# Expert first layers of two MoE blocks as pairs in the upper and lower half of TensorE's rows

## The chip, the cores and the metric

The kernel runs on one core of one Trainium2 chip. The metric is the device time of one execution in microseconds (us). TensorE (PE) multiplies, with its weight loads listed as PEld; VectorE (DVE), ScalarE (ACT) and GpSimd (POOL) do the elementwise work, SyncE (SP) issues the DMAs. PE has two clock levels, 1.2 and 2.4 GHz; the profile gives the granted clock as a share of the higher one.

## What is computed

A network of four blocks on an image batch x of shape (8, 32, 32, 64), float32, each a token mixer followed by an expert layer, with normalizations and residuals: a selective-scan mixer and dense experts; a sum-product layer and a top-2 expert layer; a sum-product layer and an LSTM; a depthwise convolution with attention and a last expert layer. The two expert layers whose first layers the change touches, and the LSTM beside which they run, are, cut to what matters:

```python
# block 1: dense experts, E = 8, 64 -> 64 -> 64 -> 64
h = jnp.einsum('bfd,edh->bfeh', x, W1) + b1
h = jax.nn.relu(_bn(h, g1, be1, m1, v1))
h = jnp.einsum('bfeh,ehk->bfek', h, W2) + b2
...
return jnp.einsum('bfed,fe->bfd', y, w)

# block 2: top-2 of 8 experts, 64 -> 128 -> 64
h = jax.nn.gelu(xf @ w1 + bb1, approximate=False)
y = h @ w2 + bb2
return (acc + we[:, None] * y, None)

# block 3: LSTM over 512 steps of a sequence, hidden size 64
i_t = jax.nn.sigmoid(xi_t + h @ V_i)
f_t = jax.nn.sigmoid(xf_t + h @ V_f)
g_t = jnp.tanh(xg_t + h @ V_c)
o_t = jax.nn.sigmoid(xo_t + h @ V_o)
c_new = h * c + i_t * g_t
h_new = o_t * jnp.tanh(c_new)
```

## The kernel before

The image is cut into 32 tiles of one image row for all 8 batches: 256 tokens, held as two groups of 128 partitions. In the first 2600 us the tiles go through a software pipeline of `turns`. In one turn each stage works on another tile: the two halves of the mixer (`block0`, `block1`) lead, the dense experts (`ffn0_*`, stage ffn) are 3 tiles ahead of the LSTM, the top-2 experts (`mix_*`, stage mix) 2 tiles, and the convolution's 49 taps (L1152) are 5 tiles behind it, so they begin five turns later. The LSTM's turn has 32 steps, each needing the step before. After this phase come the attention and the last expert layer, which the change leaves as they are.

The order of instructions on every engine is static. Each stage is a generator that yields between pieces; `weave` (L1215) merges the stages of a turn by the due times in `TIMES` (from L78), one row of numbers for each stage and engine, in half steps of the LSTM. The LSTM yields its own: its matmuls, its first tanh and the scan at t - 0.5, the second tanh and r_h at t. A piece that is due at 6 thus stands behind the matmuls of LSTM step 6 and ahead of those of step 7.

A step t of the LSTM is, by lines: three gate matmuls (L1047, L1048, L1049) read r_h and add to psL; ACT takes tanh of the gates (L1058, L1060); DVE scans the cell state (L1072); ACT takes its tanh (L1063); DVE writes the new r_h (L1077), and a scaled copy (L1079). In the text, "interval 4 to 5" is the time from the matmuls of step 4 to those of step 5 (steps are counted from 0).

The expert layers: `ffn0_pe` transposes the normalized tile f_xn (L710) into psB[0:64], ACT copies it to f_xT (L744), and the first layer multiplies it by four blocks of 128 weight columns, two experts of 64 each (L720), into the two banks of psB; ACT's relu (L755) follows. `mix_pe` does the same for m_xn (L911, ACT's copy at L952), with eight experts of 128 columns (L929) in the two banks of psC: experts 0 and 1 in bank 0, 2 and 3 in bank 1, 4 and 5 in bank 0, 6 and 7 in bank 1; ACT's gelu (L962) follows and needs its function table loaded each time. The inputs have 64 channels: partitions 64 to 127 of f_xT and m_xT hold zeros, set once, and the matmuls use all 128 rows (with `w128`, whose lower half is other data). psA belongs to the mixer, psL to the LSTM and the convolution. W holds all packed weights; a DMA named `w_late` brings those of the expert layers.

## Time and profile before

| quantity | before |
| --- | --- |
| runs | 3163.59, 3164.37, 3166.41 us; median 3164.37 |
| profiled execution | span 3157.1 us |
| PE busy | 2771.7 us, 88% |
| PEld busy | 2231.2 us, 71% |
| DVE busy | 1953.5 us, 62% |
| ACT busy | 1668.0 us, 53% |
| POOL busy | 874.9 us, 28% |
| a turn of the pipeline with convolution | about 72.7 us |

The span is the time between the first and the last instruction of the one execution that was profiled; the run times are those of other executions and include what lies around the span. A busy share is an average over stages with different limits: the pipeline of the first 2600 us has PE busy in almost all of it, the attention and the last expert layer less. In a timeline a row gives the start in us, the duration, the engine, the line, the operation, output and inputs with their shapes (for a matmul ahead of these the tile of the array, rows*columns), how many alike are merged in the row, and in brackets the idle time ahead of it and what ended that. An fp32 matmul leaves two records, an fp32 transpose one.

### The profile page before, as it was taken

How to read it: one execution, taken by the hardware profiler on the slowest of the kernel's cores; microseconds unless marked ns; L12 is line 12 of the kernel's file. 1: busy time of each engine (PE TensorE's matmuls, PEld its weight loads, DVE VectorE, ACT ScalarE, POOL GpSimd, SP SyncE). 2: the span in 40 equal slices, each digit the busy share in tenths (PEclk: the TensorE clock that was granted, in tenths of full speed). 3: DMA queues.
4: the chain of work that ended last, by engine and by line, in shares of the span. 5: the costliest groups of instructions: out<-in, count | busy, mean ns of one | idle time of the engine just before them, and what ended most of it. 6: DMA issues, size and time to landing. Idle time of an engine off the chain costs nothing. (4 is left out here: it accounts for less than half of the span.)

```text
span 3157.1 us, 64810 instructions
## 1 busy us (share of the span) xinstructions
PE 2771.7 (88%) x22240; PEld 2231.2 (71%) x22240; DVE 1953.5 (62%) x8535; ACT 1668.0 (53%) x5755; POOL 874.9 (28%) x1499
## 2 busy tenths in 40 slices
PE   4477888899999999999999999999998787887667
PEld 3366666678888788888888888788777564555556
DVE  5466666676667677777766667677754324555454
ACT  1245555566666666666665666666654423443333
POOL 2233222233233333323333333333311000000444
PEclk8677766688888888888888888888886688998888
DMA  2000000000000100000000000000000001000000
GB/s 100 14 17 18 18 19 19 19 19 19 21 21 20 32 19 19 19 19 19 19 19 19 21 21 25 27 19 19 19 17 9 3 2 28 1 1 1 8 10 11
DMA packets 54039, 59.12 MB, mean 19 GB/s; under 512 B 26576, under 2 KB 45136, under 8 KB 53328
## 3 DMA queue, kind: packets, MB, share of 16 engines
q1 hardware_dynamic: 53712, 54.99, 6.0%
q8 instruction: 177, 2.90, 0.4%
q14 instruction: 150, 1.23, 0.1%
HBM read 42.37 MB, written 4.19 MB: 15 GB/s over the span
## 5 line engine op out<-in xcount | busy, mean ns | idle before, releaser
L1072 DVE TENSOR_TENSOR_SCAN r_c<-r_wk 64x24 f32<-64x24 f32 x1024 | 244.3, 239 | 490.4 <-ACT r_wk L1058 486.5
L1058 ACT ACTIVATE r_wk<-psL 64x16 f32<-64x16 f32 x1024 | 189.1, 185 | 678.1 <-PE psL L1048 659.9
L1152 PE MATMUL psL<-img,dg 128*128 128x128 f32 x2646 | 452.7, 314 | 0.0
L1047 PEld LDWEIGHTS psL<-r_h,lv 128*64 128x64 f32 x2048 | 235.6, 162 | 291.1 <-DVE r_h L1077 162.9
L1047 PE MATMUL psL<-r_h,lv 128*64 128x8 f32 x2048 | 324.6, 231 | 80.6 <-DVE r_h L1077 74.8
L1152 PEld LDWEIGHTS psL<-img,dg 128*128 128x128 f32 x2646 | 378.4, 215 | 11.8 <-issue 3.9
L1049 PE MATMUL psL<-r_h,lv 128*64 128x8 f32 x2048 | 326.4, 232 | 0.0
L1048 PE MATMUL psL<-r_h,lv 128*64 128x8 f32 x2048 | 304.7, 222 | 0.0
L1077 DVE SCALAR_TENSOR_TENSOR r_h<-r_wk,r_tc 64x8 f32<-64x8 f32 x1024 | 196.3, 192 | 115.0 <-ACT r_tc L1063 101.5
L1063 ACT ACTIVATE r_tc<-r_c 64x8 f32<-64x8 f32 x1024 | 215.5, 210 | 83.8 <-DVE r_c L1072 37.7
L1048 PEld LDWEIGHTS psL<-r_h,lv 128*64 128x64 f32 x2048 | 252.7, 171 | 0.0
L1079 DVE SCALAR_TENSOR_TENSOR r_wk<-r_h,r_c 64x8 f32<-64x8 f32 x1024 | 223.8, 219 | 35.5
L1049 PEld LDWEIGHTS psL<-r_h,lv 128*64 128x64 f32 x2048 | 232.2, 160 | 0.0
L678 POOL TENSOR_TENSOR a_xw<-a_S,a_dtm 128x512 f32<-128x512 f32 x128 | 150.5, 1204 | 188.1 <-DVE a_dtm L591 188.1
L1060 ACT ACTIVATE r_wk<-psL 64x8 f32<-64x8 f32 x1024 | 181.7, 177 | 24.7
L929 PE MATMUL psC<-m_xT,W 128*128 128x256 f32 x512 | 167.3, 421 | 0.0
L451 PE MATMUL psA<-a_xw,a_RM 128*32 128x64 f32 x2048 | 133.1, 230 | 18.8 <-DVE state L628 17.2
L755 ACT ACTIVATE f_h<-psB,bn0b,bn0s 128x256 f32<-128x256 f32 x256 | 132.7, 556 | 8.1 <-PE psB L720 5.9
L669 POOL TENSOR_TENSOR a_bc<-W,a_S 128x128 f32<-128x128 f32 x128 | 49.5, 407 | 309.0 <-DVE a_S L565 302.0
L451 PEld LDWEIGHTS psA<-a_xw,a_RM 128*32 128x32 f32 x2048 | 113.5, 116 | 30.2 <-issue 25.9
L944 PEld LDWEIGHTS psC<-W,m_h 128*128 128x128 f32 x1024 | 130.2, 193 | 1.8
L823 PE MATMUL psC<-c_eT,accb 128*64 128x18 f32 x1024 | 129.5, 273 | 0.0
(376 smaller groups left out, 6558.8 us busy)
## 6 DMA issues: line engine op xcount, KB each, us to landing
accb<-acc_in SPq DMA_DIRECT2D x64, 512.0 KB, 4.3
a_xy<-a_E SPq DMA_DIRECT2D x512, 16.0 KB, 1.8
W<-pack_in SPq DMA_DIRECT2D x1, 3165.0 KB, 13.7
x6d<-X SPq DMA_DIRECT2D x64, 32.0 KB
out_x<-X SPq DMA_DIRECT2D x32, 64.0 KB, 1.6
X<-x_in SPq DMA_DIRECT2D x1, 1856.0 KB, 17.7
W<-pack_in SPq DMA_DIRECT2D x1, 1331.0 KB, 5.8
X<-x_in SPq DMA_DIRECT2D x1, 192.0 KB
```

The source lines that it names most:

```text
L451: last = nc.tensor.matmul(bk[TT * j:TT * j + TT].rearrange("p (b h d) -> p h b d", b=B4, h=NH)[:, h], u["RM"][:, j * NH + h], u["xw"][:, j ...
L929: last = nc.tensor.matmul(psC[:, e // 2 % 2, (e % 2) * 256:(e % 2 + 1) * 256], w128("m1w1", e * P, (e + 1) * P), u["xT"][:], start=True, s ...
L1047: nc.tensor.matmul(psL[0:64, par, c:c + LB], lv[:, 0], h, start=False, stop=False, skip_group_check=True)
L1048: nc.tensor.matmul(psL[0:64, par, c + LB:c + 2 * LB], lv[:, 1], h, start=False, stop=False, skip_group_check=True).then_inc(sem("r_z"), 1)
L1049: nc.tensor.matmul(psL[64:P, par, c:c + LB], lv[:, 2], h, start=False, stop=False, skip_group_check=True).then_inc(sem("r_zo"), 1)
L1058: nc.scalar.activation(o, psL[0:64, par, c:c + 2 * LB].rearrange("p (g b) -> p g b", b=LB), ACT.Tanh).then_inc(sem("r_gi"), 1)
L1060: nc.scalar.activation(TO, psL[64:P, par, c:c + LB], ACT.Tanh)
L1063: nc.scalar.activation(r_tc[:], r_c3[:, t % 2, 2::3], ACT.Tanh, scale=0.5).then_inc(sem("r_tc"), 1)
L1072: v.tensor_tensor_scan(r_c3[:, t % 2, :], r_wk[:, 0:24], r_wk[:, 30:54], 0.0, ALU.mult, ALU.add).then_inc(sem("r_c"), 1)
L1077: v.scalar_tensor_tensor(r_h[0:64, t + 1], TO, 1.0, r_tc[:], ALU.add, ALU.mult).then_inc(sem("r_hr"), 1)
L1079: v.scalar_tensor_tensor(r_wk[:, 32:56:3], r_h[0:64, t + 1], 0.5, r_c3[:, t % 2, 2::3], ALU.mult, ALU.mult).then_inc(sem("r_hc"), 1)
L1152: last = nc.tensor.matmul(o, dg[:, ky * KT + kx], rows[:, :, ky, kx:kx + IMG], start=(n == 0), stop=(n == KT * KT - 1))
```

## The change

The transposed tile is written twice: beside each transpose into partitions 0 to 63, a matmul with the identity writes the same into partitions 64 to 127, and ACT copies all 128 partitions. Three DMAs, issued by SP once `w_late` has landed, write weights of half of the experts into the partitions 64 to 127 that lie beside the others' weights; DVE's set-up waits for them (`w_dup`), and two memsets of the zeros leave. Each pass over the first layer is then two matmuls of 64 rows: one in rows 0 to 63 that writes bank 0, one in rows 64 to 127 that writes bank 1. For the dense experts there are two such pairs in place of four matmuls; for the top-2 layer four pairs in place of eight: experts (0,2), (1,3), (4,6), (5,7). A pair takes two due times of the table, whose numbers are unchanged, and stands at the second of them. The semaphores that tell ACT of finished banks now come with the second pair of a group, for both banks; the waits for the gate's results (f_ld, m0_ld) stand before the first pair, and the wait for a free bank before pair (4,6).

```diff
+LOWER_HALF = (("f0w1", 0, 2 * P), ("m1w1", 0, 2 * P), ("m1w1", 4 * P, 6 * P))
...
@@ ffn0_pe
             for j in range(J):
-                last = nc.tensor.transpose(psB[0:64, 0, j * P:(j + 1) * P], f_ln["xn"][:, j], ident)
+                nc.tensor.transpose(psB[0:64, 0, j * P:(j + 1) * P], f_ln["xn"][:, j], ident)
+                last = nc.tensor.matmul(psB[64:P, 0, j * P:(j + 1) * P], f_ln["xn"][:, j], ident, start=True, stop=True)
...
-            for q in range(4):
+            for q in range(2):
                 yield
-                if q == 2:
+                yield
+                if q == 0:
                     pe.wait_ge(sem("f_ld"), i1)
-                last = nc.tensor.matmul(psB[:, q // 2, (q % 2) * 256:(q % 2 + 1) * 256], w128("f0w1", q * P, (q + 1) * P), xT, start=True, stop=True)
-                if q % 2:
-                    last.then_inc(sem("f_mm1"), 1)
+                for bank in range(2):
+                    r = slice(64 * bank, 64 * bank + 64)
+                    last = nc.tensor.matmul(psB[:, bank, q * 256:(q + 1) * 256], w128("f0w1", q * P, (q + 1) * P)[r], xT[r], start=True, stop=True)
+                    if q:
+                        last.then_inc(sem("f_mm1"), 1)
@@ ffn0_act
-            nc.scalar.activation(f_xT[0:64].rearrange("p b t -> p (b t)"), psB[0:64, 0, 0:256], ACT.Copy).then_inc(sem("f_xTs"), 1)
+            nc.scalar.activation(f_xT[:].rearrange("p b t -> p (b t)"), psB[:, 0, 0:256], ACT.Copy).then_inc(sem("f_xTs"), 1)
@@ mix_pe
             for j in range(J):
-                last = nc.tensor.transpose(psC[0:64, 0, j * P:(j + 1) * P], u["ln"]["xn"][:, j], ident)
+                nc.tensor.transpose(psC[0:64, 0, j * P:(j + 1) * P], u["ln"]["xn"][:, j], ident)
+                last = nc.tensor.matmul(psC[64:P, 0, j * P:(j + 1) * P], u["ln"]["xn"][:, j], ident, start=True, stop=True)
...
-            for e in range(E):
+            for e in (0, 1, 4, 5):
                 yield
-                if e == 2:
+                yield
+                if e == 0:
                     pe.wait_ge(sem("m0_ld"), i1)
-                if e in (4, 6):
-                    pe.wait_ge(sem("m0_h"), 4 * i + (e // 2 - 1))
-                last = nc.tensor.matmul(psC[:, e // 2 % 2, (e % 2) * 256:(e % 2 + 1) * 256], w128("m1w1", e * P, (e + 1) * P), u["xT"][:],
-                                        start=True, stop=True)
-                if e % 2:
-                    last.then_inc(sem("m0_mm1"), 1)
+                if e == 4:
+                    pe.wait_ge(sem("m0_h"), 4 * i + 2)
+                for bank in range(2):
+                    r = slice(64 * bank, 64 * bank + 64)
+                    last = nc.tensor.matmul(psC[:, bank, (e % 2) * 256:(e % 2 + 1) * 256], w128("m1w1", e * P, (e + 1) * P)[r], u["xT"][r],
+                                            start=True, stop=True)
+                    if e % 2:
+                        last.then_inc(sem("m0_mm1"), 1)
@@ mix_act
-            nc.scalar.activation(u["xT"][0:64], psC[0:64, 0, 0:256], ACT.Copy).then_inc(sem("m0_xTs"), 1)
+            nc.scalar.activation(u["xT"][:], psC[:, 0, 0:256], ACT.Copy).then_inc(sem("m0_xTs"), 1)
@@ SP
+            sp.wait_ge(sem("w_late"), 16)
+            for name, upper, lower in LOWER_HALF:
+                at = COL[name][1]
+                sp.dma_start(W[64:P, at + upper:at + upper + 2 * P], pack_in[0:64, at + lower:at + lower + 2 * P]).then_inc(sem("w_dup"), 16)
@@ DVE set-up
-            v.memset(f_xT[64:P], 0.0)
-            v.memset(mix1["xT"][64:P], 0.0)
...
+                dve.wait_ge(sem("w_dup"), 16 * len(LOWER_HALF))
```

PE, around LSTM steps 4 and 5, where the dense experts' first layer stands; before, one of the four L720 is ahead of step 4 and three are behind it:

```order
L720 MATMUL psB<-f_xT,W 128x256
L1047 MATMUL psL<-r_h,lv 64x8 [waits r_hr]
L1048 MATMUL psL<-r_h,lv 64x8
L1049 MATMUL psL<-r_h,lv 64x8
L720 MATMUL psB<-f_xT,W 128x256
L720 MATMUL psB<-f_xT,W 128x256 [waits f_ld]
L720 MATMUL psB<-f_xT,W 128x256
L406 MATMUL psA<-W,hb 128x128 [waits a1_ve]
```

PE at the same place after (lines have moved by 1 to 9: the LSTM's matmuls are L1056 to L1058, the mixer's L406 is L407):

```order
L1056 MATMUL psL<-r_h,lv 64x8 [waits r_hr]
L1057 MATMUL psL<-r_h,lv 64x8
L1058 MATMUL psL<-r_h,lv 64x8
L725 MATMUL psB<-f_xT,W 128x256 [waits f_ld]
L725 MATMUL psB<-f_xT,W 128x256 x3
L407 MATMUL psA<-W,hb 128x128 [waits a1_ve]
```

All four matmuls, the two pairs, now stand behind step 4, and the wait for f_ld is ahead of all of them.

PE from LSTM step 11 to step 13, with the last expert matmuls of the top-2 layer (L736 is the dense experts' last layer, L1152 the convolution, L435 and L439 the mixer), before:

```order
L929 MATMUL psC<-m_xT,W 128x256 [waits m0_h]
L736 MATMUL psB<-W,f_h 128x128 x2
L1152 MATMUL psL<-img,dg 128x128 x3
L929 MATMUL psC<-m_xT,W 128x256
L929 MATMUL psC<-m_xT,W 128x256 [waits m0_h]
L435 MATMUL psA<-state,a_ct 128x128 [waits a1_ve]
L435 MATMUL psA<-state,a_ct 128x128
L1047 MATMUL psL<-r_h,lv 64x8 [waits r_hr]
L1048 MATMUL psL<-r_h,lv 64x8
L1049 MATMUL psL<-r_h,lv 64x8
L929 MATMUL psC<-m_xT,W 128x256
L439 MATMUL psA<-a_xy,a_bc 64x128 x2
```

And after, from the same place:

```order
L741 MATMUL psB<-W,f_h 128x128 x2
L1161 MATMUL psL<-img,dg 128x128 x3
L938 MATMUL psC<-m_xT,W 128x256 [waits m0_h]
L938 MATMUL psC<-m_xT,W 128x256
L436 MATMUL psA<-state,a_ct 128x128 [waits a1_ve]
L436 MATMUL psA<-state,a_ct 128x128
L1056 MATMUL psL<-r_h,lv 64x8 [waits r_hr]
L1057 MATMUL psL<-r_h,lv 64x8
L1058 MATMUL psL<-r_h,lv 64x8
L938 MATMUL psC<-m_xT,W 128x256 x2
L440 MATMUL psA<-a_xy,a_bc 64x128 x2
```

Ahead of step 12 three experts (4, 5 and 6) became the pair (4,6); expert 5 moved behind the matmuls of step 12, to stand with expert 7.

ACT around LSTM step 12, before; L962 is the gelu of experts 4 (with the table load ahead of it) and 5, L1058, L1060 and L1063 are the step's tanh:

```order
L962 ACT_TABLE_LOAD
L962 ACTIVATE m_h<-psC,W 128x256 [waits m0_mm1]
L1058 ACTIVATE r_wk<-psL 64x2x8 [waits r_z]
L1060 ACTIVATE r_wk<-psL 64x8 [waits r_zo]
L1063 ACTIVATE r_tc<-r_c 64x8 [waits r_c]
L962 ACTIVATE m_h<-psC,W 128x256
```

The order on ACT is the same after; what the semaphore m0_mm1 that the gelu waits for stands for is now the pair (5,7) on PE.

## Rows read from the trace of the kernel before

**Rows 1.** The page: the span, and PE's busy tenths in 40 equal slices of it.

```profile
span 3157.1 us, 64810 instructions
...
PE   4477888899999999999999999999998787887667
```

**Rows 2.** Timeline of all engines, 1400 to 1420, around LSTM steps 2 to 5.

```profile
1402.45 0.38 PE L710 MATMUL psB<-W,f_xn 128*64 128x128 f32 x2 [0.56 <-DVE f_xn L346]
...
1406.28 0.16 DVE L1077 SCALAR_TENSOR_TENSOR r_h<-r_wk,r_tc 64x8 f32<-64x8 f32 x1
...
1406.77 0.22 PE L1047 MATMUL psL<-r_h,lv 128*64 128x8 f32 x1
...
1407.10 1.56 PE L720 MATMUL psB<-f_xT,W 128*128 128x256 f32 x6
```

**Rows 3.** Timeline of all engines, 1448 to 1452, where only the LSTM chain is left.

```profile
1450.32 0.16 DVE L1077 SCALAR_TENSOR_TENSOR r_h<-r_wk,r_tc 64x8 f32<-64x8 f32 x1
...
1450.54 0.22 PE L1047 MATMUL psL<-r_h,lv 128*64 128x8 f32 x1 [0.37 <-DVE r_h L1077]
```

**Rows 4.** Timeline of PE, 1406 to 1438, LSTM steps 5, 9, 12, 13 and experts.

```profile
1410.40 0.22 PE L1047 MATMUL psL<-r_h,lv 128*64 128x8 f32 x1
...
1418.34 0.22 PE L1047 MATMUL psL<-r_h,lv 128*64 128x8 f32 x1
...
1419.44 0.60 PE L929 MATMUL psC<-m_xT,W 128*128 128x256 f32 x2
...
1426.09 1.02 PE L929 MATMUL psC<-m_xT,W 128*128 128x256 f32 x4
...
1427.49 0.22 PE L1047 MATMUL psL<-r_h,lv 128*64 128x8 f32 x1
...
1427.82 0.70 PE L929 MATMUL psC<-m_xT,W 128*128 128x256 f32 x2
...
1429.23 0.22 PE L1047 MATMUL psL<-r_h,lv 128*64 128x8 f32 x1
```

**Rows 5.** Timeline of DVE, 1404 to 1432: r_h of steps 4, 8, 11 and 12.

```profile
1409.09 0.15 DVE L1077 SCALAR_TENSOR_TENSOR r_h<-r_wk,r_tc 64x8 f32<-64x8 f32 x1
...
1418.00 0.15 DVE L1077 SCALAR_TENSOR_TENSOR r_h<-r_wk,r_tc 64x8 f32<-64x8 f32 x1
...
1426.39 0.16 DVE L1077 SCALAR_TENSOR_TENSOR r_h<-r_wk,r_tc 64x8 f32<-64x8 f32 x1
...
1428.62 0.16 DVE L1077 SCALAR_TENSOR_TENSOR r_h<-r_wk,r_tc 64x8 f32<-64x8 f32 x1
```

**Rows 6.** Timeline of ACT, 1416 to 1432: gelu, and the tanh of step 12.

```profile
1421.92 0.84 ACT L962 ACTIVATE m_h<-psC,W 128x256 f32<-128x256 f32 x2
...
1427.20 0.47 ACT L962 ACTIVATE m_h<-psC,W 128x256 f32<-128x256 f32 x1
1427.92 0.18 ACT L1058 ACTIVATE r_wk<-psL 64x16 f32<-64x16 f32 x1 [0.25 <-PE psL L1048]
```

**Rows 7.** Timeline of PE, 2712 to 2720, the attention's stage.

```profile
2713.58 1.09 PE L1602 MATMUL psL<-atT,v 128*64 128x128 f32 x16
...
2716.32 0.69 PE L1573 MATMUL psA<-k,q 64*128 64x512 f32 x1
2716.32 0.69 PE L1573 MATMUL psB<-k,q 64*128 64x512 f32 x1
2716.85 0.59 PE L1573 MATMUL psA<-k,q 64*128 64x512 f32 x1
...
2717.38 0.33 PE L1608 MATMUL psL<-W,oT 128*128 128x128 f32 x1
```

**Rows 8.** Windows of an early turn: length, busy (count) of PE, PEld, DVE, ACT, POOL; PEclk, DMA, GB/s.

```profile
540.00:544.00 4.00, 2.65 (x23) 1.99 (x22) 3.86 (x12) 3.64 (x11) 3.09 (x3) 0.98 0.00 0
544.00:547.00 3.00, 3.00 (x9) 1.43 (x10) 2.66 (x6) 2.04 (x6) 1.92 (x3) 0.50 0.00 0
547.00:550.50 3.50, 3.50 (x13) 3.01 (x12) 1.63 (x8) 2.41 (x4) 0.00 (x0) 0.50 0.00 0
```

## The prediction

> **What bounds the kernel now.** I read the page's 40 slices first: TensorE (PE) is busy in nine tenths or more of most slices of the first four fifths [rows 1]. That does not say that its work sets the time, so I read next, step by step, the timeline of one turn of the LSTM (32 steps; the one from 1396.9 us on; the 22 full turns 5 to 26 repeat it step for step). An LSTM step is a closed chain: three small matmuls (L1047 to L1049), tanh on ACT (L1058), scan on DVE, tanh (L1063), r_h on DVE (L1077), and r_h is what the next step's matmuls wait for. Where nothing else is in the way the matmul starts 0.06 us after r_h ends: 1450.48 to 1450.54 [rows 3]. Elsewhere the gap tells who is late. At step 5 r_h has been done since 1409.24 and the matmul starts at 1410.40 [rows 4, 5]: 1.16 us in which PE works off what stands ahead of it. So in the first half of a turn the interval between two LSTM steps is the PE work put between them, as far as the chain allows; what the change takes from or adds to an interval moves the whole turn, and nothing later gives it back. I therefore sum the nine intervals that the change touches, between steps 1 and 13, and count 29 turns, those in which a tile of each expert layer runs beside the LSTM. The sum is made on the profiled execution (span 3157.1 [rows 1]), which is 7.3 us under the median of the runs, 3164.4; I add the same to both.
>
> **Prices.** A 256-column fp32 matmul is two records. Two records took 0.60 at 1419.44 and four 1.02 at 1426.09 [rows 4], so a record more costs 0.21 to 0.215, a matmul 0.43, and 0.17 of every row is the tail of its last record, beside which the next line already runs. Two matmuls in rows 0 to 63 and 64 to 127 do run at the same time: the attention's L1573 starts in psA and psB both at 2716.32 [rows 7]. So a pair of experts costs 0.43, what one cost. Between tile modes there is a price: two such 512-column records in psA start 0.53 apart and the next matmul of another mode again 0.53 later (2716.32, 2716.85, 2717.38) [rows 7], where twice the 0.215 of a 256-column record is 0.43. That is 0.10 on the first record after a switch and 0.10 before the first one of the next mode. The same 0.10 is seen behind the LSTM's 128*64 matmuls, where L929 takes 0.70 against 0.60 elsewhere [rows 4]. An expert that stands right behind the LSTM has paid it already; a pair among 128*128 work pays two new ones, up to 0.4 with the first load.
>
> **Part by part, in us per turn.**
> The copies: each transpose gets a matmul beside it into partitions 64 to 127, two per tile and layer, four records of 128 columns. L1602 runs 16 such records two at a time in 1.09 [rows 7]; less the tail that is 0.12 for two, and four records in one half of the columns cost 0.47. The two transposes take 0.38 [rows 2], 0.22 without the tail. Run beside each other the copies set the time, 0.47 for 0.22: +0.25; run one behind another, +0.47. No row has a transpose beside a matmul; I take the middle, +0.36, in interval 1 (dense experts) and again in interval 2 (top-2): **+0.72**. Both intervals wait for PE, so it is all on the path. ACT's copy to SBUF has more partitions and as many elements in each: nothing.
> Interval 3 to 4: the first dense expert matmul leaves. The chain allows less than its 0.43: r_h ends at 1406.44, the LSTM starts at 1406.77 [rows 2], 0.33 against the 0.06 floor: **-0.27**.
> Interval 4 to 5: three matmuls, six records in 1.56 [rows 2], become two pairs: -0.43, plus 0.10 for the switch back and 0.06 for a load that no longer hides: **-0.27**. Both relu of ACT now wait for the second pair; LSTM step 5 has the 1.16 us above as cover, and without it up to 0.43 would show.
> Interval 6 to 7: two experts leave, a pair comes: -0.86 +0.43 +0.20 for two switches = **-0.23**; there too PE is the late one, so it counts.
> Interval 8 to 9: an expert leaves; r_h ends at 1418.15, the LSTM starts at 1418.34 [rows 4, 5]: **-0.13**.
> Interval 9 to 10: the single expert at 1419.44 [rows 4] becomes a pair among 128*128 work: two switches and a load, **+0.35**.
> Interval 11 to 12: three experts leave, a pair comes: -1.29 +0.43, and 0.36 to 0.4 for two switches: **-0.50**. r_h ended at 1426.55, 0.94 ahead of 1427.49 [rows 4, 5], so all of it counts.
> Interval 12 to 13: here a wait is added. On ACT the gelu of expert 4 stands ahead of the tanh of LSTM step 12. Before, its expert pair 4 and 5 was complete ahead of that step, and ACT ran it at 1427.20, tanh at 1427.92 [rows 6]. Now the semaphore comes only with the pair (5,7), which stands on PE behind the matmuls of step 12. From the start of these (1427.49): pair starts at +0.33 (as L929 at 1427.82), its second record +0.32, which lasts 0.38: +1.03 [rows 4]; ACT starts the gelu about 0.04 later, and the next instruction 0.37 after that (two gelu in a row take 0.84, one 0.47 [rows 6]): tanh at +1.44 where it was +0.43. What follows takes 0.86 (1427.92 to the end of r_h, 1428.78 [rows 5, 6]) and 0.06. The interval becomes 2.36, where it was 1.74 (1429.23 minus 1427.49): **+0.61**. Behind that gelu on ACT are both tanh of the step, and DVE and PE wait for them.
> At nothing I count: f_ld and m0_ld asked for earlier (both are done before the first pair's new place), the wait for a free bank before pair (4,6) (the gelu that frees it is over 2 us earlier), three 64 KB loads on SP (SP's next work is far away) and two memsets less (under half a us).
> **Sum**: 0.72 - 0.27 - 0.27 - 0.23 - 0.13 + 0.35 - 0.50 + 0.61 = +0.28 a turn, 29 turns: +8. Span 3165, time **3172**. With the copies at their ends, +0.06 to +0.50 a turn: 3166 to 3179.
>
> **Rivals.**
> *Copies strictly behind the transposes.* +0.22 a turn more than taken, 3178. For it: nothing here shows the two side by side. Against: the transposes already run in 128*64 mode [rows 2], the copies' mode. The Trainium skill, "TensorEngine Tiling (Array Packing)", section Restrictions and Gotchas, says that column tiling excludes transpose mode with fp32 input. By that rule the two would not share the array, though the trace names 128*64 for the transpose itself.
> *The clock falls in the middle of the turn.* In the early turns it does: between 540 and 544 PE was busy 2.65 of 4.00 us, and from 544 to 550.5 it had 0.50 of its clock, the 1.2 GHz level [rows 8]. The change makes such a gap: in interval 12 to 13 PE stands still for about 0.9 us, and thinner work follows (interval 13), while interval 3 to 4 loses 0.43 of work as well. Against: the gap is shorter than the 1.35 us that PE lacked in 540 to 544. The spell in these rows is 6.5 us; one half as long, 3 us, loses 1.5 us of PE work, one of 6 us 3.0. In half of 29 turns at the first price, +22; in all at the second, +87: 3194 to 3259, about 3215 for a middle.
> *Faster.* It decides on the price of a switch: if a switch costs nothing where a pair stands among other work (0.10 in interval 4, 0.20 in 6, 0.35 in 9, about 0.36 in 11) and the copies run beside the transposes (-0.22), a turn gains 0.28 - 1.01 - 0.22 = -0.95, 28 us less: 3137. It is faster than before once a switch costs under about 0.07. For it: LSTM matmuls switch modes at every step already. Against: both 0.53 spacings in rows 7.
> *The pairs don't run together.* Then six pairs cost 0.43 more each, +2.6 a turn less some cover: about 3230. Against: L1573 [rows 7].
>
> **How the numbers follow.** The sum as it stands 0.38 (3165 to 3179), copies behind 0.10 (3178), clock 0.27 (3190 to 3259), faster 0.22 (3130 to 3158), no concurrency 0.03. From 3140 to 3232 leaves out some 0.08 at the bottom and 0.10 at the top. A difference of 0.2%, 6.3 us, is about what can be told from no change: the lower quarter or more of the first case and a little of the faster one lie within it, 0.20; faster 0.21; slower the rest, 0.59.
>
> **What would show it.** In the trace after: the records of L725 and L938 start two at a time, with tile 64*128; the interval from step 12's matmuls to step 13's at 2.4 with ACT idle before the gelu of expert 4, released by PE; intervals 3, 4, 6, 8 and 11 shorter by the figures above; intervals 1 and 2 longer by 0.25 to 0.47. The forecast is wrong if interval 9 to 10 is not longer (switches are free), if interval 12 to 13 keeps 1.74 (the gelu was not in the way), or if the granted clock of 1400 to 1446 is not 1.0 throughout.

## The result, and the profile after

The changed kernel takes 3307.8 us (median of 4 runs, 3292.7 to 3311.9); the kernel before, on the same chip, 3164.0. The ratio is 1.0449, 95% interval 1.0421 to 1.0477: slower by 144 us, outside the range of the prediction (3140 to 3232). The direction was forecast, the size was not.

The page of the changed kernel: the span, and the granted clock in 40 slices (tenths of full speed); then the clock's line of the kernel before.

```profile
span 3309.7 us, 65324 instructions
...
PEclk7677575678888887888788788788776588999788
```

```profile
PEclk8677766688888888888888888888886688998888
```

The span grew by 152.6 us. Cut at the first matmul of each LSTM turn, that is: 11.7 ahead of turn 0; 35.6 in the turns 0 to 4, which have no convolution; 81.6 in the 22 turns 5 to 26; 23.7 in the turns 27 to 30, which have the convolution whole (98 records of L1152 in each, before) while the mixer ends (with half its work in turn 27) and then the dense experts (with turn 28); nothing in turn 31 and behind it. In the turns 5 to 26 two kinds stand side by side. Fifteen turns have full clock from step 3 to step 21, as all 22 had before, and are 0.9 us longer each (14.1 in all). Seven fall to half clock at step 13 and are 5 to 12 us longer (67.5 in all, some 61 of it beyond the 0.9 of every turn). At the end of a turn the clock falls in every turn of both kernels, somewhere between step 22 and step 25, and comes back in step 0 or 1 of the next turn. So there are two things to explain: a small loss in every turn, and the falls at step 13.

**In every turn: intervals 1 and 2.** PE in turn 15 of the changed kernel, first the transposes (L711) and copies (L712) of the dense experts' tile, then the first layer as pairs (L725).

```profile
1472.28 0.27 PE L711 MATMUL psB<-W,f_xn 128*64 128x128 f32 x1
1472.48 0.43 PE L712 MATMUL psB<-W,f_xn 128*64 128x128 f32 x2
1472.84 0.30 PE L711 MATMUL psB<-W,f_xn 128*64 128x128 f32 x1
1473.07 0.43 PE L712 MATMUL psB<-W,f_xn 128*64 128x128 f32 x2
1473.43 0.25 PE L397 MATMUL psA<-bias,ones 65*128 65x168 bf16 x1
1473.61 0.22 PE L1056 MATMUL psL<-r_h,lv 128*64 128x8 f32 x1
...
1478.57 1.14 PE L725 MATMUL psB<-f_xT,W 64*128 64x256 f32 x8
```

Before, the two transposes stood at 1402.45 in one row of 0.38 [rows 2], and the next line began 0.29 later:

```profile
1402.74 0.23 PE L396 MATMUL psA<-bias,ones 65*128 65x168 bf16 x1
```

Now it is 1.15 from the first transpose to the next line: 0.20 and 0.23 from a transpose to its copy, 0.36 from a copy to what follows. At 0.11 a record (in e3 below, records of one column half start 0.11 apart) a transpose is 0.11 and a copy's two records 0.22, so every change between the two kinds adds 0.09 to 0.14, on top of the work, and no copy starts beside a transpose. The L725 row shows the pairs as forecast: eight records of 64 rows in 1.14, where six of 128 rows took 1.56 [rows 2]; the two of a pair start 0.01 apart.

**At step 12.** ACT, then PE, at the matmuls of steps 12 and 13 of the same turn; the brackets give the idle time ahead and what ended it.

```profile
1499.36 0.47 ACT L971 ACTIVATE m_h<-psC,W 128x256 f32<-128x256 f32 x1 [1.15 <-PE psC L938]
1499.74 0.17 ACT L1067 ACTIVATE r_wk<-psL 64x16 f32<-64x16 f32 x1
```

```profile
1498.30 0.22 PE L1056 MATMUL psL<-r_h,lv 128*64 128x8 f32 x1
...
1498.63 0.70 PE L938 MATMUL psC<-m_xT,W 64*128 64x256 f32 x4
...
1500.63 0.22 PE L1056 MATMUL psL<-r_h,lv 128*64 128x8 f32 x1 [0.51 <-DVE r_h L1086]
```

The gelu (L971) waits 1.15 for the pair (5,7), the tanh comes 1.44 after the step's matmuls, and the interval is 2.33, where it was 1.74 (rows 4, 1427.49 and 1429.23): the stall of the prediction, to 0.03 us.

**The falls.** Windows of turn 15 of the kernel before (intervals 12 and 13), of turn 15 of the changed kernel (intervals 12, 13 and 14 with 15), and then of the same place in turn 16, which has a fall; columns as in [rows 8].

```profile
1427.49:1429.23 1.74, 1.74 (x15) 1.10 (x14) 1.06 (x5) 1.23 (x5) 0.00 (x0) 1.00 0.04 9
1429.23:1432.65 3.42, 3.42 (x33) 2.99 (x32) 3.07 (x9) 2.70 (x6) 2.92 (x4) 1.00 0.00 0
```

```profile
1498.30:1500.63 2.33, 1.82 (x18) 1.10 (x17) 0.81 (x6) 1.16 (x5) 0.00 (x0) 1.00 0.00 0
1500.63:1504.04 3.41, 3.41 (x31) 2.99 (x31) 2.80 (x10) 2.83 (x7) 2.51 (x3) 1.00 0.00 0
1504.04:1508.88 4.84, 4.84 (x63) 4.11 (x62) 2.87 (x15) 1.94 (x8) 2.59 (x6) 1.00 0.02 3
```

```profile
1571.68:1574.01 2.33, 1.81 (x18) 1.10 (x17) 0.81 (x6) 1.16 (x5) 0.00 (x0) 1.00 0.00 0
1574.01:1577.72 3.71, 3.71 (x32) 2.99 (x32) 2.81 (x10) 2.83 (x7) 2.81 (x4) 0.91 0.00 0
1577.72:1586.27 8.55, 8.55 (x62) 7.18 (x62) 2.88 (x15) 1.93 (x8) 3.34 (x7) 0.50 0.00 0
```

The two turns of the changed kernel have the same instructions in the same order; in turn 16 the clock goes to 0.50, the 1.2 GHz level, inside interval 13, and intervals 14 and 15 take 8.55 in place of 4.84. It comes back only some 24 us later: turn 16 is 84.6 us long, turn 15 73.6. Which turn falls is not told by its instructions. All seven falls begin at the same place, inside interval 13, 35.8 to 36.7 us behind the first matmul of the turn; in the experiments below it is 34.5 to 36.9 us, and inside interval 13 each time.

### The profile page after: what moved, and what is told of

Same layout as the page of the kernel before. It is cut to its first block and busy times, and to the rows that moved or that the text cites. A ratio compares the mean times of both kernels' runs of the same rounds, so it can differ in the third digit from the quotient of the medians.

```text
span 3309.7 us, 65324 instructions
## 1 busy us (share of the span) xinstructions
PE 2899.0 (88%) x22496; PEld 2273.7 (69%) x22496; DVE 1924.6 (58%) x8533; ACT 1659.1 (50%) x5755; POOL 873.1 (26%) x1499
## 5 line engine op out<-in xcount | busy, mean ns | idle before, releaser
L1081 DVE TENSOR_TENSOR_SCAN r_c<-r_wk 64x24 f32<-64x24 f32 x1024 | 221.5, 216 | 577.9 <-ACT r_wk L1067 575.8
L1161 PE MATMUL psL<-img,dg 128*128 128x128 f32 x2646 | 472.2, 324 | 0.0
L1056 PEld LDWEIGHTS psL<-r_h,lv 128*64 128x64 f32 x2048 | 239.5, 165 | 321.2 <-DVE r_h L1086 209.8
L1056 PE MATMUL psL<-r_h,lv 128*64 128x8 f32 x2048 | 329.3, 233 | 106.8 <-DVE r_h L1086 99.6
L1161 PEld LDWEIGHTS psL<-img,dg 128*128 128x128 f32 x2646 | 394.8, 224 | 13.1 <-issue 5.8
L1058 PE MATMUL psL<-r_h,lv 128*64 128x8 f32 x2048 | 330.8, 234 | 0.0
L1057 PE MATMUL psL<-r_h,lv 128*64 128x8 f32 x2048 | 309.3, 224 | 0.0
L1057 PEld LDWEIGHTS psL<-r_h,lv 128*64 128x64 f32 x2048 | 259.1, 175 | 0.0
L1088 DVE SCALAR_TENSOR_TENSOR r_wk<-r_h,r_c 64x8 f32<-64x8 f32 x1024 | 216.5, 211 | 35.6
L1058 PEld LDWEIGHTS psL<-r_h,lv 128*64 128x64 f32 x2048 | 236.6, 163 | 0.0
L452 PE MATMUL psA<-a_xw,a_RM 128*32 128x64 f32 x2048 | 164.0, 261 | 16.4 <-DVE state L629 15.1
L452 PEld LDWEIGHTS psA<-a_xw,a_RM 128*32 128x32 f32 x2048 | 141.0, 136 | 29.2 <-issue 25.6
L953 PEld LDWEIGHTS psC<-W,m_h 128*128 128x128 f32 x1024 | 154.5, 224 | 2.8
L953 PE MATMUL psC<-W,m_h 128*128 128x64 f32 x1024 | 151.4, 301 | 0.0
L971 ACT ACTIVATE m_h<-psC,W 128x256 f32<-128x256 f32 x256 | 113.2, 471 | 41.6 <-PE psC L938 39.5
## 6 DMA issues: line engine op xcount, KB each, us to landing
W<-pack_in SPq DMA_DIRECT2D x1, 3165.0 KB, 14.1
```

What stands on the lines that cost most here:

```text
L452: last = nc.tensor.matmul(bk[TT * j:TT * j + TT].rearrange("p (b h d) -> p h b d", b=B4, h=NH)[:, h], u["RM"][:, j * NH + h], u["xw"][:, j ...
L953: last = nc.tensor.matmul(psC[:, j, e * C:(e + 1) * C], u["h"][:, e, j * P:(j + 1) * P], w("m1w2", e * C, (e + 1) * C), start=False, stop= ...
L1056: nc.tensor.matmul(psL[0:64, par, c:c + LB], lv[:, 0], h, start=False, stop=False, skip_group_check=True)
L1057: nc.tensor.matmul(psL[0:64, par, c + LB:c + 2 * LB], lv[:, 1], h, start=False, stop=False, skip_group_check=True).then_inc(sem("r_z"), 1)
L1058: nc.tensor.matmul(psL[64:P, par, c:c + LB], lv[:, 2], h, start=False, stop=False, skip_group_check=True).then_inc(sem("r_zo"), 1)
L1081: v.tensor_tensor_scan(r_c3[:, t % 2, :], r_wk[:, 0:24], r_wk[:, 30:54], 0.0, ALU.mult, ALU.add).then_inc(sem("r_c"), 1)
```

## The experiments

All ratios are against the kernel before on the same chip, with 95% intervals. "Falls" are falls to half clock at step 13 in the 22 turns 5 to 26. Falls and idle time are those of the one profiled execution, the time is the median of all runs; other executions of a kernel can have other counts (the four runs of f1 took 3187.7 to 3231.2 us).

| kernel | time, us | ratio | falls | PE idle in interval 12 |
| --- | --- | --- | --- | --- |
| changed | 3307.8 | 1.0449 [1.0421, 1.0477] | 7 | 0.51 |
| e1 copies alone | 3230.3 | 1.0209 [1.0182, 1.0236] | 0 | 0 |
| e2 copies by ACT | 3230.2 | 1.0211 [1.0180, 1.0242] | 3 | 0.51 |
| e3 plain matmuls for both halves | 3280.7 | 1.0371 [1.0331, 1.0411] | 9 | 0.51 |
| e4 pair (5,7) ahead of step 12 | 3307.2 | 1.0456 [1.0399, 1.0514] | 7 | 0.26 |
| f1 the pairs' places, not paired | 3197.7 | 1.0140 [1.0080, 1.0201] | 2 | 0.09 |
| f2 e2 with three taps moved | 3187.2 | 1.0090 [1.0060, 1.0119] | 0 | 0 |
| f3 transposes ahead of copies | 3347.7 | 1.0592 [1.0545, 1.0639] | 14 | 0.51 |
| f4 f2 with e4's edit | 3164.1 | 1.0005 [0.9984, 1.0025] | 0 | 0 |
| g1 f4, paired in turns 5 to 26 only | 3129.0 | 0.9896 [0.9876, 0.9915] | 0 | 0 |
| g2 changed, with three taps moved | 3255.9 | 1.0283 [1.0244, 1.0322] | 0 | 0 |
| g3 before, with three taps moved | 3163.9 | 0.9996 [0.9983, 1.0009] | 0 | 0 |
| h1 changed, one tap cut in six | 3440.9 | 1.0888 [1.0825, 1.0951] | 20 | 0 |

### What a copy costs: e1, e3, f3

e1 adds the copies to the kernel before, unread (here and in e3 and f3 the edit is shown for the dense experts; the top-2 layer has the same):

```diff
-                last = nc.tensor.transpose(psB[0:64, 0, j * P:(j + 1) * P], f_ln["xn"][:, j], ident)
+                nc.tensor.transpose(psB[0:64, 0, j * P:(j + 1) * P], f_ln["xn"][:, j], ident)
+                last = nc.tensor.matmul(psB[64:P, 0, j * P:(j + 1) * P], f_ln["xn"][:, j], ident, start=True, stop=True)
```

> The kernel before with the four copies alone (the matmuls with the identity into partitions 64 to 127); the first layers stay as before, nothing reads the copies. Theory A (a transpose and a matmul can't share the array and every change between them is paid, so a copy costs what it costs whatever stands around it): intervals 1 and 2 grow by 0.95 to 1.05 us each as in the changed kernel, all 29 turns, +55 to +60: about 3222, and the clock in steps 3 to 22 stays full in the turns 5 to 26. Theory B (the copies are what lets the clock fall): the same growth, and half clock from step 13 in some of the turns 5 to 26 as in the changed kernel: 3270 or more. My first sum (+0.36 each) would give 3185.

Measured 3230.3. Interval 1 went from 2.28 to 3.24, interval 2 from 2.25 to 3.29, the others up to 22 stayed, and no turn fell at step 13. The rows repeat those of the changed kernel (PE, turn 14 of e1):

```profile
1367.29 0.27 PE L710 MATMUL psB<-W,f_xn 128*64 128x128 f32 x1
1367.49 0.43 PE L711 MATMUL psB<-W,f_xn 128*64 128x128 f32 x2
1367.86 0.30 PE L710 MATMUL psB<-W,f_xn 128*64 128x128 f32 x1
```

So the copies alone cost 2.0 us in the two intervals and 66 us in all, and alone they do not make the falls. The 22 turns 5 to 26 are only 1.5 us longer each (33.6 in all), because intervals 23 and 24, where the clock falls in every turn, became shorter; the rest of the span's 72.4 lies ahead of turn 0 (11.1), in the turns 0 to 4 (13.6) and 27 to 30 (8.5), and behind them (5.7).

e3 writes both halves with plain matmuls and no transpose:

```diff
-                nc.tensor.transpose(psB[0:64, 0, j * P:(j + 1) * P], f_ln["xn"][:, j], ident)
+                nc.tensor.matmul(psB[0:64, 0, j * P:(j + 1) * P], f_ln["xn"][:, j], ident, start=True, stop=True)
```

> The changed kernel with the transposes replaced: both halves are written by plain matmuls with the identity, one in columns 0 to 63 and one in columns 64 to 127. Theory A (what costs is the change between transpose and matmul): the two halves run beside each other as the LSTM's do, four records, 0.47 to 0.5 in place of 1.15: intervals 1 and 2 shrink by 0.6 to 0.7 each, 29 turns, -36 to -40: about 3270 if the falls of the clock stay. Rival (the copies run one behind another because they share weights or input): eight records in a row, 0.95 to 1.0: no more than 10 us less.

PE of e3, the same place in turn 9:

```profile
1026.46 0.32 PE L711 MATMUL psB<-W,f_xn 128*64 128x128 f32 x1
1026.47 0.32 PE L712 MATMUL psB<-W,f_xn 128*64 128x128 f32 x1
1026.62 0.27 PE L711 MATMUL psB<-W,f_xn 128*64 128x128 f32 x1
...
1027.05 0.25 PE L397 MATMUL psA<-bias,ones 65*128 65x168 bf16 x1
```

The two halves start 0.01 apart: they run beside each other, and it is 0.59 to the next line in place of 1.15. Interval 2 is 2.59 (3.29 in the changed kernel), as theory A has it. Interval 1 is not: 3.08 against 3.19. The tile's own time fell there too, by the 0.56 of the rows, but more of the interval ran at half clock (its mean granted clock is 0.77 against 0.91). The time, 3280.7, is 27 us less in place of 36 to 40, with two falls more.

f3 puts both transposes of a tile ahead of both copies:

```diff
             for j in range(J):
                 nc.tensor.transpose(psB[0:64, 0, j * P:(j + 1) * P], f_ln["xn"][:, j], ident)
+            for j in range(J):
                 last = nc.tensor.matmul(psB[64:P, 0, j * P:(j + 1) * P], f_ln["xn"][:, j], ident, start=True, stop=True)
```

> The changed kernel with both transposes of a tile ahead of both copies. Theory A (each change between transpose and matmul costs 0.10 to 0.14): two changes fewer in interval 1 and in interval 2, 0.2 to 0.28 less each: intervals 2.95 and 3.05 in place of 3.19 and 3.29, -12 to -16 us with the same falls of the clock. Rival (a copy costs what it costs because of its weight load): no change of the intervals. The time itself also moves with the number of falls, so the intervals decide.

PE of f3, turn 9: the two transposes, the four records of the copies, the next line.

```profile
1034.62 0.38 PE L711 MATMUL psB<-W,f_xn 128*64 128x128 f32 x2
1034.94 0.65 PE L713 MATMUL psB<-W,f_xn 128*64 128x128 f32 x4
1035.52 0.25 PE L397 MATMUL psA<-bias,ones 65*128 65x168 bf16 x1
```

0.90 in place of 1.15, and interval 2 went from 3.29 to 3.02: two changes fewer, 0.13 each, with as many records and weight loads as before. The sum of a copy is thus settled: its records, run alone, and 0.09 to 0.14 for every change between transpose and matmul. The time went up all the same, to 3347.7, because 14 turns fell: a cheaper order of PE took 40 us more, by the clock.

### Where the falls come from: e2, e4, f1

e2 takes the copies off PE; ACT writes the lower half too (for the top-2 layer alike):

```diff
+            nc.scalar.activation(f_xT[64:P].rearrange("p b t -> p (b t)"), psB[0:64, 0, 0:256], ACT.Copy).then_inc(sem("f_xT2"), 1)
```

> The changed kernel without the copies on PE: ACT writes the transposed tile twice, into partitions 0 to 63 and 64 to 127. Theory A (copies cost 1.0 us each on PE, the clock falls for another reason, the wait in interval 12 to 13): intervals 1 and 2 return to 2.3 and 2.25, the falls from step 13 on stay in a third of the turns: 3308 - 58 = 3250. Theory B (the copies bring about the falls, by the thinner work or by their place in time): the falls go too, and what is left is the pairs' gain of 0.27 + 0.23 + 0.23 + 0.19 + 0.47 less 0.40 and 0.59, that is -0.4 us a turn: about 3152.

3230.2: between the two. The 15 turns with full clock from step 3 to step 22 take 72.1 us on average (72.7 before), so pairs without copies on PE do gain there, though ACT's second copy makes intervals 1 and 2 some 0.2 longer than before. Three turns fall at step 13 and four more have a short spell of 3.4 us at step 4; the turns 0 to 4 are 20.6 us longer than before. The profiled execution is the fastest of the four (3216.6; the others 3227 to 3237).

e4 changes one due time, so that pair (5,7) stands ahead of step 12:

```diff
-        (1.5, 2.5, 5.5, 6, 7.5, 9, 10.5, 11, 11, 11.5, 12.5, ...
+        (1.5, 2.5, 5.5, 6, 7.5, 9, 10.5, 11, 11, 11, 12.5, ...
```

> The changed kernel with one number of the table changed: pair (5,7) is due at 11 and so stands behind pair (4,6), ahead of the matmuls of step 12. Theory A (the wait of the tanh of step 12 for the gelu, and PE's standstill of 0.9 us there, let the clock fall): interval 12 to 13 is 1.4 or less, interval 11 to 12 is 0.5 longer, ACT no longer waits there, and the turns 5 to 26 keep full clock up to step 22: 0.1 to 0.5 us a turn less and the 58 us of the falls in the turns 5 to 26, about 3235 to 3250 with the early turns as they are. Rival (the falls come from less work in all, or from the copies): the falls stay, 3295 to 3305.

The gelu no longer delays the tanh, and interval 12 is 1.34. But 7 turns fall, and the time is the same. Windows of e4, intervals 12, 13 and 14 with 15 of turn 14:

```profile
1427.50:1428.85 1.35, 1.09 (x14) 0.72 (x13) 0.66 (x4) 0.80 (x4) 0.00 (x0) 1.00 0.00 0
1428.85:1432.69 3.84, 3.84 (x31) 3.09 (x31) 2.81 (x10) 2.83 (x7) 2.94 (x4) 0.88 0.00 0
1432.69:1441.25 8.56, 8.56 (x63) 7.19 (x62) 2.78 (x15) 1.93 (x8) 2.62 (x7) 0.50 0.01 3
```

My theory that ACT's wait makes the falls is wrong. PE still stands idle in that interval, for 0.26 us, now waiting for the LSTM's chain itself, so e4 leaves standstill and thin work mixed.

f1 is the kernel before with its full 128-row matmuls in the pairs' places, order and waits, without copies:

```diff
-            for e in range(E):
+            for e in (0, 1, 4, 5):
                 yield
+                yield
...
+                for bank in range(2):
+                    b = e + 2 * bank
+                    last = nc.tensor.matmul(psC[:, bank, (e % 2) * 256:(e % 2 + 1) * 256], w128("m1w1", b * P, (b + 1) * P), u["xT"][:], start=True, stop=True)
```

> The kernel before (no copies, no pairs) with its first-layer matmuls moved to where the changed kernel has its pairs, in the pairs' order and with their waits and semaphores: two 128-row matmuls one after the other in each place. The gelu of expert 4 waits behind step 12 as in the changed kernel, for 0.43 longer. Theory A (the falls at step 13 come from thin PE work in intervals 11 to 13, which the pairs make by doing two matmuls in the time of one): no falls in the turns 5 to 26, since the same places hold twice the work; intervals 4 and 9 are 0.4 longer than before, 3, 8 and 11 shorter, interval 12 is 2.8: 29 times about +1.0: 3190 to 3195. Rival B (the standstill of PE while ACT waits for the semaphore lets the clock fall): falls at step 13 in a third or more of the turns 5 to 26, 3250 or more.

Windows of f1, intervals 12 and 13 of turn 14, one of two turns with a fall:

```profile
1360.79:1363.13 2.34, 2.25 (x18) 1.48 (x17) 0.75 (x5) 1.16 (x5) 0.00 (x0) 1.00 0.00 0
1363.13:1367.04 3.91, 3.91 (x32) 3.17 (x32) 2.81 (x10) 2.83 (x7) 2.99 (x4) 0.86 0.00 0
```

3197.7 is near theory A's time, but by luck: the turns with full clock are 0.2 us longer than before, not 1.0, and the rest is two falls (19 us) and the stretches outside the turns 5 to 26. Since two turns fell, neither theory is met as I put it. Interval 12 was 2.34, not 2.8, and PE was idle in it for only 0.09. With twice the matmul work in the same places the falls become rare, but not absent.

### Filling the place: f2, g2, g3, h1

f2 is e2 with the three convolution taps due at 11 moved to 12 (two numbers of the table):

```diff
-        (0, 0, 0, 0.5, 0.5, 7, 8.5, 8.5, 9.5, 10, 11, 11, 12, 13.5, ...
+        (0, 0, 0, 0.5, 0.5, 7, 8.5, 8.5, 9.5, 10, 12, 12, 12, 13.5, ...
```

> The kernel with the copies by ACT (e2) and two numbers of the table changed: the three convolution taps that were due at 11 are due at 12, where PE otherwise stands still, behind step 12 and the pair (5,7). Theory A (thin work in intervals 12 and 13 makes the falls): the three falls of e2 at step 13 in the turns 5 to 26 go, and interval 11 is 0.6 shorter at no cost in interval 12: 71.2 a turn, 3164 - 29 x 1.2 plus some us in the turns without convolution: 3130 to 3150. Rival C (the falls come from less work in all over a turn, wherever it stands): three or more falls stay, 3200 or more.

No turn from 5 to 26 falls at step 13 (one has a short spell at step 4); these turns sum to 1579 us, against 1617 in e2 and 1600 before. The total, 3187.2, is above the 3130 to 3150 that I expected, because the turns 0 to 4 and 27 to 30 lose 22 and 23 us against before.

g2 is the same edit on the changed kernel and nothing else.

> The changed kernel with one edit: the three taps due at 11 are due at 12, into PE's standstill. Theory A (thin work in intervals 12 and 13 makes the falls): no falls at step 13 in the turns 5 to 26, 73.1 a turn or less there (interval 11 is 0.6 shorter), so the 65 us of falls and some 12 more go: 3225 to 3235; the falls of the turns 0 to 4 and 27 to 29 stay. If the falls have to do with the copies: they stay, 3290 or more.

Windows of g2, intervals 12, 13 and 14 with 15 of turn 15:

```profile
1483.49:1485.92 2.43, 2.43 (x24) 1.78 (x23) 1.59 (x8) 1.84 (x6) 0.00 (x0) 1.00 0.00 0
1485.92:1489.33 3.41, 3.41 (x33) 2.98 (x32) 2.71 (x10) 2.74 (x7) 2.61 (x4) 1.00 0.00 0
1489.33:1494.16 4.83, 4.83 (x62) 4.10 (x61) 2.92 (x15) 1.93 (x8) 2.45 (x5) 1.00 0.01 3
```

All 22 turns have full clock there; 3255.9, 52 us less than the changed kernel for two numbers of a table. It is 20 us more than expected. About half of that lies in the turns 5 to 26, which are 73.6 us each in place of 73.1: intervals 11 and 12 are 0.6 shorter than in the changed kernel, but intervals 1, 23 and 24, where the clock changes in every turn, take it back. The gain is thus the falls alone. The turns 0 to 4 stay as slow as in the changed kernel (426 and 425, against 390 before).

g3 is the same edit on the kernel before.

> The kernel before with the same edit to the table and nothing else, to tell what of a gain is the taps' and what the pairs'. Interval 11 is 0.65 shorter (r_h is 0.94 ahead there), interval 12, where PE is 0.46 late only, takes 0.65 more work: +0.25 to +0.65 there. So 0 to -0.4 in each of 22 turns: 3154 to 3164; no falls.

3163.9, ratio 0.9996: interval 11 is 0.67 shorter and interval 12 0.67 longer. The taps by themselves are worth nothing; they pay only where the pairs have left PE room.

Does PE's standstill let the clock fall, or the little that it has to do? h1 cuts the one tap that stands in interval 12 of the changed kernel into six matmuls over parts of its columns:

```diff
+                    if n == 21:
+                        for b0, t0, t1 in ((0, 0, 16), (0, 16, 32), (1, 0, 16), (1, 16, 32), (2, 0, 32), (3, 0, 32)):
+                            nc.tensor.matmul(o[:, b0, t0:t1], dg[:, ky * KT + kx], rows[:, b0, ky, kx + t0:kx + t1], start=False, stop=False)
```

> The changed kernel with the one convolution tap that stands in interval 12 to 13 cut into six matmuls over parts of its 128 columns: the same columns and products, but twelve records in place of two, so that PE is busy for about 0.5 us longer in the place where it stood still. It tells two readings of the falls at step 13 apart. Reading A (PE's standstill itself lets the clock fall): PE's idle time in interval 12 goes from 0.51 to 0.1 or less, the falls at step 13 go from the turns 5 to 26, about 3235 to 3250. Reading B (what counts is how much the array has to do, not whether it is busy): the same columns are still too few, and falls stay in a quarter or more of the turns 5 to 26: 3290 to 3330. Interval 12 may be up to 0.3 us longer, at most 7 us in all.

Windows of h1, turn 18: interval 12, and what follows.

```profile
1793.27:1796.05 2.78, 2.78 (x27) 2.21 (x27) 1.25 (x7) 1.41 (x5) 0.00 (x0) 1.00 0.02 6
1796.05:1799.50 3.45, 3.45 (x30) 3.34 (x30) 3.05 (x9) 2.69 (x6) 3.00 (x4) 0.77 0.00 0
```

PE is busy through the whole of interval 12, and 20 of 22 turns fall; 3440.9 us (three runs of 3423 to 3455, one of 3511). So a fall does not need a standstill in interval 12. In g2 eight records of whole taps fill the same interval and nothing falls; here twelve records of pieces of one tap fill it and nearly everything does. Reading A is refuted. Reading B fits better, but not in size: the columns are those of the changed kernel, which fell in 7 turns, and only the interval is longer, by 0.45.

### Put together: f4, g1

f4 joins f2 with e4's due time, and moves ACT's second copy of the top-2 tile behind the second tanh of step 2:

```diff
             nc.scalar.activation(u["xT"][0:64], psC[0:64, 0, 0:256], ACT.Copy)
+            yield
             nc.scalar.activation(u["xT"][64:P], psC[0:64, 0, 0:256], ACT.Copy).then_inc(sem("m0_xTs"), 1)
```

> As f2, and pair (5,7) ahead of step 12 (as in e4), and ACT's second copy of the top-2 layer behind the second tanh of step 2. Theory A: interval 12 is limited by the chain or by four taps, 1.4 to 1.8, intervals 11 and 12 together 4.5 in place of 5.13 before, interval 2 back at 2.25: about 70.4 a turn; the four taps keep interval 12 dense, so no falls at step 13: 3105 to 3130. If the falls come back: 3180 or more.

The turns 5 to 26 sum to 1567.5 (1599.8 before), with intervals 11 and 12 at 4.36 together, interval 2 back at 2.245 and no falls. The total is that of before, 1.0005, and 34 us above what I expected: the turns 0 to 4 give back 18.4 and the turns 27 to 30 15.7, and the profiled execution lost 9 more behind them.

g1 therefore pairs only in the 22 full turns (what I call the turns without the full convolution there are the turns 0 to 4, which have none, and the turns 27 to 30, which have it whole but lack the mixer):

```diff
+        def in_pairs(turn):
+            return 5 <= turn <= 26
...
-            for e in (0, 1, 4, 5):
+            for e in (0, 1, 4, 5) if pairs else ():
...
+            for e in () if pairs else range(E):
```

> As f4 (copies by ACT, pair (5,7) ahead of step 12, three taps from interval 11 to 12), but with the first layers as in the kernel before in all turns without the full convolution (before turn 5 and after turn 26), where f4 had its additional falls; partitions 64 to 127 are zero there again. If thin PE work is what lets the clock fall and nothing else of f4 costs time: turns 5 to 26 as f4, 71.2 each (1567), turns 0 to 4 and 27 to 30 as before (390 and 257), 280 ahead and 631 behind: span 3125, time 3125 to 3135, 1% faster than before. If the copies by ACT or the table cost something in the early turns too: 3140 to 3150.

3129.0 us, ratio 0.9896 [0.9876, 0.9915]: 1% less than before, clear of the interval, and within what was expected. Its page, and its windows of intervals 12 and 13 in turn 15:

```profile
span 3124.1 us, 64882 instructions
...
PEclk9677786778888888888888888888886588998888
```

```profile
1404.19:1405.88 1.69, 1.69 (x20) 1.40 (x19) 1.32 (x7) 1.56 (x6) 0.00 (x0) 1.00 0.04 10
1405.88:1409.29 3.41, 3.41 (x33) 2.98 (x32) 3.21 (x9) 2.67 (x6) 2.77 (x4) 1.00 0.00 0
```

Turns 5 to 26 sum to 1565.0, 34.8 less than before. Against f4, which pairs there too, the turns 0 to 4 went from 408.1 to 377.1 and the turns 27 to 30 from 272.6 to 258.5. Against before, the turns 0 to 4 are 12.6 shorter (of the edits to the table only expert 7's due time reaches them, and no run has it alone; in g3, whose edit does not reach them, they are 3.4 shorter too); 7.5 ahead of turn 0 and 5.5 behind turn 30 are lost (g3 has 5.6 more there as well).

## Why the prediction was wrong, point by point

Two steps of the sum failed. It took the granted clock as full wherever it summed, and left the clock to a rival with spells of 6 us at most; the runs showed spells of 7 to 24 us in seven of 22 turns (67 us longer), and the turns 0 to 4 and 27 to 30, where stages of the pipeline are missing, became 59 us longer. And it sized the copies at +0.72 a turn, where they cost +1.95 in their two intervals. The copies alone would have left the time at about 3211 or less, inside the range; the clock took it out.

Medians of the turns with full clock, in us; the intervals not listed moved by less than 0.02, apart from 23 and 24, where the clock falls in every turn. It comes back in interval 0 or 1 in most, so the figure for interval 1 varies from turn to turn (its mean change in the fifteen turns is +0.87).

| interval | before | after | change | forecast |
| --- | --- | --- | --- | --- |
| 1 | 2.28 | 3.19 | +0.91 | +0.36 |
| 2 | 2.25 | 3.29 | +1.04 | +0.36 |
| 3 | 1.62 | 1.35 | -0.27 | -0.27 |
| 4 | 3.63 | 3.40 | -0.23 | -0.27 |
| 6 | 2.48 | 2.24 | -0.23 | -0.23 |
| 7 | 2.05 | 2.12 | +0.07 | 0 |
| 8 | 1.85 | 1.65 | -0.20 | -0.13 |
| 9 | 2.60 | 3.00 | +0.40 | +0.35 |
| 11 | 3.38 | 2.92 | -0.47 | -0.50 |
| 12 | 1.75 | 2.33 | +0.59 | +0.61 |

- **The pairs, their switches, the wait at step 12: right.** Without the copies the sum was -0.44 a turn, measured -0.34. The price of 0.10 a switch, read off the attention's rows [rows 7], held in the intervals 4, 6, 9 and 11; the stall at step 12 came to 0.59 for 0.61.
- **The copies: the step that failed first.** I bounded them by 0.25 (beside the transposes) and 0.47 (behind them) and took the middle. They cost 0.91 and 1.04 (0.96 and 1.04 in e1). The upper bound held only the records; I charged a switch where rows of the array are divided and forgot it between a transpose and a matmul in tiles of the same size. One row could be read either way: L1608, one record for an fp32 operation, is a transpose, and stood 0.53 behind a matmul that takes 0.43 [rows 7]; I put the 0.10 down to the change of tile, from 64*128 to 128*128, which stands there too. Corrected, the sum is +1.6 a turn in place of +0.28, 39 us more: about 3211. ACT's wider copy, counted at nothing, is nothing: 0.384 for 128 partitions, 0.377 for 64.
- **"Nothing later gives it back": wrong by some 0.6 a turn.** The intervals of the table add up to +1.6, and the same turns are only 0.9 longer. Intervals 23 and 24 are together 0.55 shorter, because the clock falls later against the steps (mean granted clock 0.99 and 0.74 there, 0.75 and 0.51 in the same turns before). In e1 the same two intervals give 0.4 back.
- **The rival "copies strictly behind the transposes": right in kind, wrong in price.** The Trainium skill, "TensorEngine Tiling (Array Packing)", section Restrictions and Gotchas, had said that column tiling and fp32 transposes exclude each other. The trace agrees so far that L711 and L712 never start less than 0.20 apart, while e3's matmuls in the same two halves start 0.01 apart; but it names 128*64, a column tile, for the transposes too. The price, +0.22 a turn in the prediction, was +1.2.
- **The clock: the right rival, sized too small.** I gave it 27% and 22 to 87 us for all 29 turns. The seven turns with a fall at step 13 are 67 us longer by themselves. I had counted spells of 3 to 6 us in half or all turns; they last 7 to 24 us, in a third of them. And I had priced the turns 0 to 4 and 27 to 30, where less stands between the LSTM's steps, like the others: they are 59 us longer. The copies alone (e1) have 22 of these (13.6 and 8.5), the pairs without copies on PE (e2) 36 (20.6 and 15.4), 58 together. The mean granted clock of the turns 0 to 4 is 0.70 before, 0.69 in e1, 0.65 in e2 and 0.63 in the changed kernel; in g1, which does not pair there, it is 0.73.
- **Its mechanism as I put it fell.** I named the standstill at step 12 (0.9 us; it measured 0.51). e4 removed ACT's stall, left PE idle for 0.26, and kept the falls; h1 removed the standstill and made them worse; f2, f4, g1 and g2 filled the place with whole taps and had none. The pairs halve the time that PE spends on the first layers, and around steps 12 and 13 what is left is thin. That this thin work lets the clock fall is argued from these runs, not shown.
- **What stays open.** f1 fell twice with the work of before in the pairs' places. f3 changes intervals 1 and 2 alone and doubles the falls, to 14: how many turns fall also depends on edits far ahead of step 13, which thin work around it does not explain. Why turn 16 falls and turn 15 does not, with the same instructions, no run shows. The 11.7 us ahead of turn 0 are much like the 11.1 of e1, where only the copies were added.

## What to carry to other kernels

Where TensorE's clock depends on what it does, less work in a stretch is not simply time gained: look, before an edit that thins PE's work, for the thinnest stretch it leaves and for real work that can be moved there; in this kernel two numbers of a table took 52 us off the changed kernel. Price every change of mode of the array, that between transpose and matmul included, at the gap that the rows show (0.09 to 0.14 here), and put work of one mode together, or let another engine write the second copy. A sum by intervals can be right to 0.1 us per turn in most of its terms (here all but the copies) and still miss the time by 136 us: where the clock changes in a turn, what one interval gains or loses is partly taken back in another, and a fall costs more than all terms together. Read the clock of each turn before the sum is trusted.

## What the runs showed of the hardware

- A transpose and a matmul in tiles of the same size, 128*64, cost 0.09 to 0.14 us at each change between them, and never started less than 0.20 us apart; two matmuls in the two column halves started 0.01 us apart.
- A record over 16 or 32 columns took nearly as long as one over 128. In h1 the twelve records over 16 and 32 columns fill the time from 1794.60 to the next step's matmul at 1796.05, 0.12 each; in g2 the eight records over 128 columns fill 1484.83 to 1485.91, 0.135 each. I had expected interval 12 of h1 to grow by 0.3 at most; it grew by 0.45. PE of h1, turn 18 (the row names the first shape of its group):

```profile
1794.60 1.52 PE L1163 MATMUL psL<-img,dg 128*128 128x16 f32 x12
1796.05 0.22 PE L1056 MATMUL psL<-r_h,lv 128*64 128x8 f32 x1
```

- With PE busy through the whole of interval 12 the clock fell behind it all the same, in 20 of 22 turns (h1); with four whole taps there in place of the pieces it stayed at 1.00 in 22 of 22 (g2).
- ACT's copy of 256 columns took 0.377 us from 64 partitions (before) and 0.384 from 128 (changed kernel).
